# Two attention layers: context and query projections in half-precision parts, feed-forward tiles moved, and stacked queries and keys copied from tile to tile in SBUF

## The chip, the cores and the metric

The kernel runs on one core of one Trainium2 chip. The metric is the device time of one execution in microseconds. Engine names: TensorE (PE), VectorE (DVE), ScalarE (ACT), GpSimd (POOL), and SyncE (SP), which here only issues DMAs.

## What is computed

The batch has 64 sequences of 128 tokens, x with 320 channels and a context with 192 channels (its last 4 tokens are image tokens). Layer 0 is an attention with 8 heads of 40 channels, layer 1 a transformer block with 20 heads of 16:

```python
# layer 0
query, keyt, valt = x @ Wq, enc @ Wk, enc @ Wv            # enc: the first 124 context tokens
hs = mha(query, keyt, valt, 8)                            # "first"
ca_q1 = einsum('btc,th->bch', ca, Wq_ca)[:, indices, :]   # ca: the last 4
ca_hs1 = mha(ca_q1, x, x, 8)                              # "ca"
ca_hs2 = mha(ca_hs1 @ Wq, ca @ Wk_ca, ca @ Wv_ca, 8)
x = (hs + ca_hs2) @ Wout + b_out + x
# layer 1
h = ln(x);  x = attn(h, h, q1, k1, v1, 20) @ o1_w + o1_b + x          # "self"
h = ln(x);  x = attn(h, context, q2, k2, v2, 20) @ o2_w + o2_b + x    # "cross"
h = ln(x);  a, g = split(h @ ff_w1 + ff_b1)
out = a * gelu(g) @ ff_w2 + ff_b2 + x
```

## The kernel before

A step works on G = 2 sequences (256 tokens). It is one pass of a hardware loop (`Fori(0, STEPS + 1)`, 33 passes) on each engine, and the passes are software-pipelined: while pass i does the "ca" and self-attention of tile i, its cross-attention and the "first" attention, it also does the feed-forward part (`ff0` to `ff9`, `y0`, `y1`) of the tile before. After the loop a tail does the last tile's feed-forward part.

**The order is written out by hand**, once for each engine, and checked against one list of jobs, `BODY`. A job is one use of a PSUM bank: job n uses bank n mod 6 (`j_bank`), TensorE may fill it once the last reader of job n - 6 is done (`bank_free`), ScalarE reads it first, then VectorE (`a_done`, `v_done`). Two more banks (`o_bank`) hold the attention outputs.

Names of jobs: `Q0T0..2`, `K0T0..2`, `K1T`, `Q1T`, `Q2T`, `K2T` are chunks of transposed queries and keys for the first, self and cross attention; `V0`, `V1`, `V2` values; `S0..S27` scores of four heads each, `mx0..7` the turned maxima of a group, `T0..T27` the exponents (transposed scores with the maxima subtracted). Units 0 to 3 are "ca" (two for each sequence), 4 to 13 self, 14 to 23 cross, 24 to 27 first. For each `T` ScalarE computes two exponentials (in float32 to `P`, and in float16 to `PT`), GpSimd the low half `PT[1] = P - PT[0]` (`low_probabilities`, L519), and `attend` multiplies both with the values. `outT`/`outM` are the turned outputs and the output projection, `XT` the turned norm (`hTn`, `hT3` in the code, written by `high_blocks` L699 and `low_blocks` L1051 to L1054), `G` the token gains, `mT`/`mB` the extremes of the next tile over all partitions, `s4`, `p4T`, `hs` the small attention over 4 tokens, `caT` its turned queries.

**Precision.** Most matmuls multiply float16 parts: a value is split in a high half (ScalarE) and a low half, and `PASSES` lists eight products of 128 rows or fewer that cover 320 input rows. The projections from x (`Wq`) and from the context (`Wk`, `Wv`, `k2`, `v2`) are float32 matmuls instead (`transposed`, `values`), three input chunks for x and two for the context. A float32 matmul shows as two instructions in the trace.

**Stacking.** Scores need the high and low halves of queries and keys stacked on the partitions, one block of 16 or 40 rows for each part and one column block for each head (`Qs`, `Ks`, `Q0s`, `K0s`). The chunks `cQ` and `cK` are laid out otherwise. So SP stores each chunk to DRAM (`put`, L371) and, after the last chunk of a tensor, loads the stack back in three DMAs (`stack`, L375):

```python
def put(src, k, r, dst, at, landed):
    sp.dma_start(dst[:, at:at + r, :].rearrange("a p n -> p a n"), src[0:r, :, k, :]).then_inc(landed, 16)

def stack(dst, src, e, parts, landed):
    for y, part in enumerate(parts):
        sp.dma_start(dst[y * e:(y + 1) * e, :, :],
                     src[part, :, :].rearrange("(h e) n -> e h n", e=e)).then_inc(landed, 16)
```

Scores of a group wait for its whole stack (`self_stacked`, `first_stacked`, `cross_stacked`). SP also loads the next tile (`load_next`), in its place in one queue.

**The start** finds the largest weight (a maximum and a minimum of each matrix on VectorE), scales and splits the weights, computes bias shifts (`ff_shifts`: 20 tiles), and computes for all tiles the products of `Wk_ca` and `Wq` (`M4`), which go to DRAM in one DMA from ScalarE's queue. VectorE then clears buffers that lie over the staging area, and the loop begins.

## Time and profile before

| | us |
|---|---|
| median of 3 runs | 3950.0 (3941.24 to 3958.27) |
| the profiled execution: time | 3965.49 |
| its span, first to last instruction | 3963.6 |
| TensorE busy | 3580.9 (90%) |
| VectorE, ScalarE, GpSimd busy | 2308.9 (58%), 2268.7 (57%), 1966.4 (50%) |
| mean granted TensorE clock | 0.966 |

The busy time of TensorE includes modelled ends of pipelined matmuls, so what a group of matmuls costs is read from the start of the group to the start of the next. The span is read in three parts: the start, the 33 passes, the tail.

### The profile page before, as it was taken

The page shows a single profiled execution, that of the slowest core. Times are in us where ns is not written, and L with a number is a line of the kernel's source. Part 1 is how long each engine was busy: PE and PEld are TensorE (multiplying, and loading weights), DVE is VectorE, ACT ScalarE, POOL GpSimd, SP SyncE. Part 2 cuts the span into 40 slices and gives each one's busy share as a digit, 9 for nine tenths or more (in the row PEclk, how much of TensorE's full clock was granted, in tenths as well). Part 3 has the DMA queues.
Part 4 walks back from the last instruction along what each step waited for, and adds up shares of the span by engine and source line. Part 5 has one row for each costly group of instructions (what it writes and reads, how often), then busy time and mean ns, then how long its engine had stood idle before and what let it go on. Part 6 is the DMA issues. An engine that isn't in the chain of part 4 may idle for free.

```text
span 3963.6 us, 112057 instructions
## 1 busy us (share of the span) xinstructions
PE 3580.9 (90%) x38314; PEld 2867.6 (72%) x38314; DVE 2308.9 (58%) x5535; ACT 2268.7 (57%) x4084; POOL 1966.4 (50%) x2229
## 2 busy tenths in 40 slices
PE   6499999999999999999999999999999999999999
PEld 5377777777777777777777777777777777777777
DVE  6466556556555655655556556555655656556555
ACT  2356655665556556556655665566566556655664
POOL 0345444554555445555554554545445555554553
PEclk9799999999999999999999999999999999999999
DMA  4332333222233332232333322233332232333321
GB/s 138 63 61 53 58 61 66 59 46 60 59 55 61 67 61 49 53 65 51 63 63 66 59 46 60 56 58 61 67 64 47 53 64 53 63 63 66 59 46 42
DMA packets 417600, 238.71 MB, mean 60 GB/s; under 512 B 44315, under 2 KB 416715, under 8 KB 416843
## 3 DMA queue, kind: packets, MB, share of 16 engines
q1 hardware_dynamic: 405317, 229.62, 29.6%
q8 instruction: 366, 6.00, 0.7%
q10 hardware_dynamic: 11910, 3.04, 0.3%
...
## 4 chain that ended last, share of the span: by engine, by line
PE 36%; issue 30%; POOL 17%; DVE 5%; SPq 4%; DMA 3%; ACT 3%; POOLq 1%; ACTq 0%; DVEq 0%
PE bank L1412 35%; POOL PT L519 10%; DMA xin<-in_x 3%; DVE mx L1025 2%; ACT PT L742 2%; POOL cQ L526 2%; POOL XA L496 1%; POOL cK L526 1%; SPq L365 1%; POOL rstd L566 1%; SPq L363 1%; POOL XB L496 1%; PE bank L1446 1%; PE bank L1531 1%; SPq L361 1%
## 5 line engine op out<-in xcount | busy, mean ns | idle before, releaser
L519 POOL TENSOR_TENSOR PT<-P,PT 128x512 f16<-128x512 f32 (+1 forms) x924 | 1068.8, 1157 | 642.1 <-ACT PT L742 640.8
L1412 PE MATMUL bank<-hT,w_ff_w 128*128 128x256 f16 x5440 | 651.6, 277 | 1.7 <-DVE hT L1054 1.7
L1025 DVE TENSOR_REDUCE mx<-bank 128x4 f32<-128x512 f32 (+1 forms) x924 | 579.6, 680 | 104.4 <-PE bank L1412 96.5
L1412 PEld LDWEIGHTS bank<-hT,w_ff_w 128*128 128x128 f16 x5440 | 532.5, 100 | 73.2 <-issue 6.5
L1412 PE MATMUL bank<-mxs,pick 84*128 84x128 f16 (+1 forms) x3696 | 513.4, 220 | 0.0
L1412 PE MATMUL bank<-w_ff,F 128*128 128x320 f32 x1360 | 411.5, 442 | 1.3 <-DVE F L1104 1.3
L1412 PEld LDWEIGHTS bank<-mxs,pick 84*128 84x128 f16 (+1 forms) x3696 | 375.1, 103 | 16.8 <-issue 8.2
L1412 PEld LDWEIGHTS bank<-V,PT 128*128 128x128 f16 (+1 forms) x9504 | 314.5, 96 | 84.0 <-POOL PT L519 37.9
L723 ACT ACTIVATE P<-bank,ff_b,scale 128x256 f32<-128x256 f32 x340 | 187.8, 562 | 324.9 <-PE bank L1412 285.4
L1412 PE MATMUL bank<-Qs,Ks 96*128 96x128 f16 x2640 | 361.7, 220 | 0.1
L1412 PE MATMUL bank<-V,PT 128*128 128x17 f16 (+1 forms) x9504 | 343.7, 172 | 17.1 <-POOL PT L519 14.3
L1104 DVE SCALAR_TENSOR_TENSOR F<-bank,ff_b,P 128x256 f32<-128x256 f32 x340 | 163.3, 483 | 266.5 <-ACT P L723 262.7
L741 ACT ACTIVATE P<-bank,log_p,held 128x512 f32<-128x512 f32 x330 | 256.2, 776 | 80.7 <-PE bank L1412 42.8
L1412 PEld LDWEIGHTS bank<-w_ff,F 128*128 128x128 f32 x1360 | 242.4, 190 | 78.0 <-DVE F L1104 1.5
L565 POOL TENSOR_TENSOR rstd<-mv,eps 128x1 f32<-128x1 f32 x198 | 41.4, 209 | 502.8 <-DVE mv L1092 502.8
L741 ACT ACTIVATE P<-bank,log_p,exp_self 128x512 f32<-128x512 f32 x330 | 255.6, 775 | 45.0 <-PE bank L1412 42.8
L1412 PEld LDWEIGHTS bank<-Qs,Ks 96*128 96x128 f16 x2640 | 253.2, 98 | 20.9 <-issue 6.0
L1071 DVE RECIPROCAL rden<-bank 128x20 f32<-128x20 f32 (+1 forms) x264 | 63.2, 239 | 345.0 <-PE bank L1412 345.0
L526 POOL TENSOR_TENSOR cQ<-whole,cQ 128x256 f16<-128x256 f32 (+1 forms) x198 | 131.9, 667 | 257.8 <-DVE whole L929 254.2
L741 ACT ACTIVATE P<-bank,log_p,factor 124x512 f32<-124x512 f32 (+1 forms) x264 | 204.9, 776 | 93.4 <-PE bank L1412 87.7
L742 ACT ACTIVATE PT<-bank,log_p,held 128x512 f16<-128x512 f32 x330 | 254.6, 772 | 0.0
L742 ACT ACTIVATE PT<-bank,log_p,exp_self 128x512 f16<-128x512 f32 x330 | 254.4, 771 | 0.0
...
## 6 DMA issues: line engine op xcount, KB each, us to landing
Ks<-scratch_k SPq DMA_DIRECT2D x198, 160.0 KB, 4.5
Qs<-scratch_q SPq DMA_DIRECT2D x198, 160.0 KB, 5.7
...
Q0s<-scratch_q SPq DMA_DIRECT2D x99, 160.0 KB
K0s<-scratch_k SPq DMA_DIRECT2D x99, 160.0 KB
...
```

The lines of the kernel that those rows point to most:

```text
L361: sp.dma_start(cT2[0:r, k, :], d["cT"][before, k * r:(k + 1) * r, :]).then_inc(step_loaded, 16)
L496: nc.gpsimd.tensor_tensor(dst[:, b, :], src[:, b, :], bias[:, j, :], ALU.add).then_inc(ready, 1)
L519: nc.gpsimd.tensor_tensor(PT[0:keys, n % PT_SLOTS, 1, :], P[0:keys, n % P_SLOTS, :], PT[0:keys, n % PT_SLOTS, 0, :], ALU.subtract).then_in ...
L526: nc.gpsimd.tensor_tensor(dst[0:r, 1, k, :], whole[0:r, m % 3, :], dst[0:r, 0, k, :], ALU.subtract)\
L565: link(i, nc.gpsimd.tensor_tensor(rstd[:, j, b:b + 1], mv[:, j, b, 1:2], eps[:, :], ALU.add))
L723: nc.scalar.activation(gate[:, t % 2, :], bank[:, 0:GS], ACT.Gelu, scale=scale[:, 1:2], bias=ff_b[:, FFT + t:FFT + t + 1]).then_inc(a_done, 1)
L741: nc.scalar.activation(P[0:keys, n % P_SLOTS, :], bank[0:keys, :], ACT.Exp, bias=log_p[0:keys, :], scale=by)
L742: nc.scalar.activation(PT[0:keys, n % PT_SLOTS, 0, :], bank[0:keys, :], ACT.Exp, bias=log_p[0:keys, :], scale=by).then_inc(a_done, 1)
L1025: nc.vector.tensor_reduce(mx[:, g % 2, 4 * u:4 * u + 4], bank[:, :].rearrange("p (h s) -> p h s", h=4)[:, :, 0:keys], axis=AX.X, op=ALU.ma ...
L1071: link(i, nc.vector.reciprocal(rden[:, g % 4, 0:heads].unsqueeze(2), o[:, :, e:e + 1]))
L1104: nc.vector.scalar_tensor_tensor(out=F[:, t, :], in0=bank[:, GS:2 * GS], scalar=ff_b[:, t:t + 1], in1=gate[:, t % 2, :], op0=ALU.add, op1= ...
L1412: return nc.tensor.matmul(o, lhsT, rhs, start=start, stop=stop)
```

## The change

- `Wq`, `Wk`, `Wv`, `k2`, `v2` become split float16 weights like the others (`MATS16`), with new pass lists of eight products for x and five for the context. x and the context of a tile are split on chip: ScalarE scales them in place and takes the high halves (`split_x`, `split_context`), GpSimd the low halves (`low_x`, `low_context`).
- `Qs`, `Ks`, `Q0s`, `K0s` are filled by DMAs from `cQ` and `cK` directly, chunk by chunk (`spread`), for all but the cross keys. The columns of `Wq`, `Wk`, `q1`, `k1`, `q2` are permuted on the host for that. Each chunk has a semaphore of its own; a score unit waits for the chunks that hold its heads, and ScalarE's write over a chunk of `cQ` or `cK` waits for the copies out of it.
- The orders change: `ff0` to `ff3` come before `T0` and `ff4` to `ff7` around the end of the self-attention; `gate` is a buffer of its own, no longer part of `P`; `K0T`, `K2T`, `V0`, `S`, `outM` and others move; SP loads the next tile after the copies of `Q1T` and before those of `K0T`.
- At the start: one reduction with absolute values for each matrix, the products `M4` earlier and in four parts, each written to DRAM by itself, buffers cleared by GpSimd, the loads for the token products first.

The core of the diff:

```diff
+PASSES_C = ((1, 0, 0), (3, 0, 0), (1, 1, 0), (2, 0, 1), (2, 1, 1))
+PASSES_X = ((1, 0, 0), (1, 1, 0), (4, 0, 0), (2, 0, 1), (2, 1, 1), (5, 0, 1), (3, 0, 2), (3, 1, 2))
...
 BODY = jobs_of("""
-    Q0T0 XT0_0 Q0T1 XT0_1 Q0T2 K1T0 K1T1 K1T2 Q1T0 Q1T1 Q1T2 S0 S1 V0_0 V1_0 mx0 S2 S3 T0 K0T0 T1
-    V1_1 mx1 K0T1 T2 S4 S5 S6 S7 S8 T3 vca mx2 S9 S10 T4 S11 S12 T5 S13 caT0 T6 mx3 T7 T8 caT1 K0T2
-    T9 T10 T11 T12 T13 V0_1 outT1_0 ff0 ff1 outM1_0 outT1_1 ff2 ff3 outM1_1 XT1_0 ff4 s4 XT1_1 ff5
-    Q2T0 Q2T1 Q2T2 ff6 ff7 mT ff8 mB ff9 S14 S15 S16 S17 y1 S18 S19 mx4 S20 S21 S22 T14 S23 K2T0 T15
-    mx5 S24 T16 S25 T17 T18 T19 T20 S26 T21 mx6 T22 outT2_0 S27 y0 T23 p4T T24 mx7 T25 outM2_0 K2T1
-    T26 hs0 T27 outT2_1 V2_0 outT0_0 hs1 K2T2 outM2_1 outT0_1 XT2_0 V2_1 outM0_0 outM0_1 XT2_1 G
+    Q0T0 XT0_0 XT0_1 S0 Q0T1 Q0T2 K1T0 K1T1 K1T2 Q1T0 Q1T1 Q1T2 S1 ff0 S2 S3 ff1 ff2 mx0 K0T0 ff3 T0
+    V1_0 K0T1 mx1 K0T2 V0_0 T1 V1_1 T2 S4 S5 S6 S7 S8 T3 vca mx2 S9 T4 S10 T5 S11 T6 S12 S13 caT0
+    mx3 T7 T8 T9 T10 T11 T12 T13 caT1 ff4 outT1_0 ff5 ff6 ff7 outT1_1 outM1_0 outM1_1 ff8 XT1_0 ff9
+    XT1_1 s4 Q2T0 Q2T1 Q2T2 mT mB V0_1 K2T0 K2T1 y1 S14 S15 S16 S17 S18 mx4 S19 S20 T14 S21 T15 S22
+    S23 T16 S24 S25 mx5 T17 S26 T18 S27 mx6 T19 T20 T21 T22 p4T T23 T24 mx7 outT2_0 T25 y0 T26
+    outM2_0 V2_0 outT2_1 T27 hs0 outM2_1 outT0_0 hs1 XT2_0 V2_1 outT0_1 outM0_0 K2T2 outM0_1 XT2_1 G
...
+            def spread(name, k, dst, src, e, rows, parts):
+
+                heads = rows[k] // e
+                at = rows[0] // e * k
+                for y, part in enumerate(parts):
+                    sp.dma_start(dst[y * e:(y + 1) * e, at:at + heads, :], src[0:rows[k], part, k, :])\
+                        .then_inc(stacked[name][k], 16)
...
-            def put_low(i, name, k, src, rows, dst, at, landed, behind=None):
+            def put_low(i, name, k, dst, src, parts):
+                if (name, k) == ("Q0T", 0):
+                    sp.wait_ge(j_full, done(i - 1, LOOP_JOBS.number("T27"), "J"))
                 sp.wait_ge(v_done, v_job(i, LOOP_JOBS, f"{name}{k}"))
-                if behind is not None:
-                    sp.wait_ge(behind, i * STACK_LOADS + STACK_LOADS)
-                put(src, k, rows[k], dst, at[k], landed)
+                spread(name, k, dst, src, D0, CH0, parts)
...
+            def low_x(i):
+
+
+                pool.wait_ge(x_high, i + 2)
+                nc.gpsimd.tensor_tensor(x16[:, 3:6, :], xT[:, :, :], x16[:, 0:3, :], ALU.subtract).then_inc(x16_ready, 1)
+
+            def low_context(i):
+
+                pool.wait_ge(c_high, i + 1)
+                nc.gpsimd.tensor_tensor(c16[:, 2:4, :], cT[:, :, :], c16[:, 0:2, :], ALU.subtract).then_inc(c16_ready, 1)
...
+            def split_x(i):
+
+                act.wait_ge(step_loaded, i * LOADS_STEP + 2 * LOADS_STEP)
+                act.wait_ge(next_ready, i + 2)
+                act.wait_ge(j_full, done(i, LOOP_JOBS.number("Q0T2"), "J"))
+                nc.scalar.activation(xT[:, :, :], xT[:, :, :], ACT.Copy, scale=next_factor[:, SX:SX + 1])\
+                    .then_inc(x_scaled, 1)
+                act.wait_ge(x_scaled, i + 2)
+                nc.scalar.activation(x16[:, 0, :], xT[:, 0, :], ACT.Copy, scale=lower[:, :])
+                nc.scalar.activation(x16[:, 1:3, :], xT[:, 1:3, :], ACT.Copy).then_inc(x_high, 1)
...
-                        pe.wait_ge({SELF: self_stacked, CROSS: cross_stacked, FIRST: first_stacked}[att],
-                                   i * STACK_LOADS + STACK_LOADS)
+                elif b == 0 and att != CA:
+
+                    per = CH0[0] // D0 if att == FIRST else CH1[0] // D1
+                    for c in range(-(-4 * u // per), (4 * u + 3) // per + 1):
+                        if att == CROSS:
+                            pe.wait_ge(stacked["Q2T"][c], i * STACK_LOADS + 2 * STACK_LOADS)
+                        else:
+                            for name in (("K0T", "Q0T") if att == FIRST else ("K1T", "Q1T")):
+                                pe.wait_ge(stacked[name][c], i * STACK_LOADS + STACK_LOADS)
```

## Rows read from the trace of the kernel before

**Rows 1.** The page: busy time, share of the span, and instructions of each engine.
```profile
PE 3580.9 (90%) x38314; PEld 2867.6 (72%) x38314; DVE 2308.9 (58%) x5535; ACT 2268.7 (57%) x4084; POOL 1966.4 (50%) x2229
```

**Rows 2.** TensorE in order of time: start, duration, line, operation, count, idle before.
```profile
152.12 2.91 PE L1412 MATMUL bank<-xT,w_Wq 120*120 120x256 f32 x6 [4.34 <-DVE G L942]
...
1989.07 1.56 PE L1412 MATMUL bank<-xT,w_Wq 120*120 120x256 f32 x6 [1.59 <-DVE hT L1054]
...
2035.42 0.46 PE L1412 MATMUL bank<-V,PT 128*128 128x17 f16 x12 [0.44 <-POOL PT L519]
...
2061.78 1.06 PE L1412 MATMUL bank<-Ks,Qs 96*128 96x128 f16 x16
...
2088.57 0.25 PE L1412 MATMUL bank<-Q0s,K0s 120*124 120x128 f16 x1
...
2102.47 1.56 PE L1412 MATMUL bank<-xT,w_Wq 120*120 120x256 f32 x6 [1.59 <-DVE hT L1054]
...
3930.92 17.63 PE L1412 MATMUL bank<-hT,w_ff_w 128*128 128x256 f16 x160 [1.68 <-DVE hT L1054]
```

**Rows 3.** What TensorE waited for: total us, times, longest.
```profile
PE bank L1412 <- POOL PT L519: 105.1, 99, 1.6
PE bank L1531 <- DVE mx L1025: 56.8, 126, 1.2
PE bank L1412 <- DVE hT L1054: 52.6, 33, 1.7
...
PE bank L1412 <- DMA Qs<-scratch_q: 9.3, 19, 1.3
```

**Rows 4.** Two neighbouring passes: length, busy time per engine, granted clock, DMA share, GB/s.
```profile
269.00:381.60 112.60, 104.03 (x1147) 83.33 (x1147) 67.07 (x163) 67.68 (x122) 59.21 (x67) 0.98 0.31 57
381.60:498.83 117.23, 106.97 (x1146) 84.74 (x1146) 67.15 (x163) 67.69 (x122) 59.23 (x67) 0.96 0.29 57
```

**Rows 5.** TensorE in order of time: groups of matmuls and what follows them.
```profile
2051.12 3.67 PE L1412 MATMUL bank<-hT,w_ff_w 128*128 128x256 f16 x32
2054.63 0.27 PE L1638 MATMUL bank<-ident,ext_wide 128*128 128x128 f32 x1
...
2067.94 1.08 PE L1412 MATMUL bank<-cT,w_k 96*128 96x256 f32 x4
2068.86 0.22 PE L1412 MATMUL bank<-Qs,Ks 96*128 96x128 f16 x1
...
2095.73 1.24 PE L1412 MATMUL bank<-w_v,cT 96*128 96x320 f32 x4
2096.81 2.34 PE L1412 MATMUL bank<-w_Wout,hTn 128*128 128x320 f16 x16
2099.05 0.54 PE L1446 MATMUL bank<-ident,OB 128*128 128x128 f32 x3
```

**Rows 6.** Groups of ScalarE's instructions: count, busy us, mean ns, idle before.
```profile
L741 ACT ACTIVATE P<-bank,log_p,exp_self 128x512 f32<-128x512 f32 x330 | 255.6, 775 | 45.0 <-PE bank L1412 42.8
...
L723 ACT ACT_TABLE_LOAD x34 | 43.6, 1283 | 0.6
```

**Rows 7.** Groups of GpSimd's instructions: the low half of the probabilities.
```profile
L519 POOL TENSOR_TENSOR PT<-P,PT 128x512 f16<-128x512 f32 x792 | 915.9, 1156 | 615.4 <-ACT PT L742 614.1
```

**Rows 8.** SP's queue in order of time: three DMAs of a stack.
```profile
2028.39 1.30 SPq L375 DMA_DIRECT2D Ks<-scratch_k  x3
```

**Rows 9.** DMA issues: count, KB each, median us from issue to landing.
```profile
Ks<-scratch_k SPq DMA_DIRECT2D x198, 160.0 KB, 4.5
```

**Rows 10.** TensorE, VectorE and GpSimd at the start, in order of time.
```profile
46.79 29.14 PE L1412 MATMUL bank<-ln_b,raw_ff_w 128*128 128x1 f32 x120
...
125.62 0.59 DVE L1236 MEMSET X<- 128x640 f32 x1 [35.61 <-DMA scratch_M<-M_all]
...
150.35 0.72 POOL L541 TENSOR_TENSOR X<-xin,next_factor 128x320 f32<-128x320 f32 x1 [149.91 <-ACT next_factor L761]
...
157.12 3.60 POOL L558 TENSOR_TENSOR ca_heads<-ca,mask_ca 96x2048 f16<-96x2048 f16 x1
```

More of the change, by code:

```diff
@@ L308, in build @@
         split_done = sem("split_done")
-        self_put, q0_put, k0_put = sem("self_put"), sem("q0_put"), sem("k0_put")
-        q2_put, k2_put = sem("q2_put"), sem("k2_put")
-        self_stacked, first_stacked, cross_stacked = sem("self_stacked"), sem("first_stacked"), sem("cross_stacked")
+        stacked = {n: [sem(f"{n}_stacked{k}") for k in range(3)] for n in ("Q0T", "K0T", "Q1T", "K1T", "Q2T")}
+        k2_put, cross_stacked = sem("k2_put"), sem("cross_stacked")
         vx_ready, ca_ready = sem("vx_ready"), sem("ca_ready")
@@ L1845, in _ @@
[L1845 to L1851 removed]
+                attend(i, 22)
+                exponents(i, 25)
+                ff_part(i, 0, 8, 10)
                 attend(i, 23)
                 exponents(i, 26)
[L1854 removed]
+                out_proj(i, 2, 0)
+                values(i, "V2", 0, "v2")
```

862 lines of the change are left out of this document (455 added, 407 removed).

## The prediction

> **What bounds the kernel now.** I read the page first, for the shares of the engines; then what TensorE waited for; then the trace in order of time for one tile, to see what each stretch of the loop hangs on; then the start. TensorE is busy 90% of the span, ScalarE and VectorE under 60%, GpSimd 50% [rows 1]. The first matmul of the loop starts at 152.1 us, the last tile's work ends where the tail begins, at 3930.9, and the span ends at 3963.6 [rows 2]. So the time is start 152.1, 33 passes of 3778.8 / 33 = 114.5 us, tail 32.7. The profiled execution took 3965.5 us, 0.4% over the median of 3950.0; the sum is made against it and scaled at the end.
>
> One pass, from 1989.07 to 2102.47, took 113.4 us [rows 2]. I cut it at three points where the reader can see the order of the work: the end of the self-attention's last product (2035.9: it starts at 2035.42 and the next group 0.4 later), the first cross score (2061.78), and the last exponents of the first attention, T27 (2088.57). That gives A = 46.8, B = 25.9, C = 26.8, D = 13.9 us. TensorE's waits [rows 3] are mostly on GpSimd's low half of the probabilities, 105.1 us in all or 3.2 per pass, on VectorE's maxima (1.7) and at the head of each pass on the bank that VectorE's split of hT empties (1.6). The wait for the stacked queries is small: 9.3 us in 19 waits.
>
> The clock matters too. Of two neighbouring passes with the same instructions one took 112.6 at a mean granted clock of 0.98 and the other 117.2 at 0.96 [rows 4]: in both TensorE is at 1.2 GHz for a part of the pass and at 2.4 for the rest, and passes differ by that part.
>
> **The change, part by part.** *Projections in half precision.* Per pass 21 single-precision matmuls of 256 columns (Wq 9, Wk and k2 6 each) and 8 of 320 (Wv, v2) go. Two of the first kind take 2068.86 - 2067.94 = 0.92 us, two of the second 2096.81 - 2095.73 = 1.08 [rows 5]. In their place come 8 half-precision matmuls for each chunk of Wq and 5 for the others. A 256-column one costs 3.51 / 32 = 0.11 us (2051.12 to 2054.63), a 320-column one 2.24 / 16 = 0.14 [rows 5]. So Wq gives 3 x (1.38 - 0.88) = 1.5, Wk and k2 6 x (0.92 - 0.55) = 2.2, Wv and v2 4 x (1.08 - 0.70) = 1.5: 5.2 us of TensorE per pass. At the busy share of 90% most of it counts where TensorE sets the pace, none where ScalarE does.
>
> *The splits that this needs.* ScalarE gets six copies over 768, 256 and 512, and 512, 256 and 256 elements. The exponentials cost 0.775 for 512 [rows 6]; that bounds the six from above at 3.9 us (2560 elements), and nothing bounds them from below but the same row without its fixed part; I take 3. GpSimd gets subtractions over 768 and 512 elements: at 1.156 for 512 [rows 7], 2.9 us. The context's split stands between two chunks of Q0T, where ScalarE has half of each chunk's 0.9 us free; x's stands in the ten us before the cross scores; GpSimd does one during the projections and one after its last probabilities. I charge 0 to 0.5 us.
>
> *Feed-forward tiles moved.* Four of the ten move ahead of T0, four to the end of the self-attention. They fill the holes in A, but Gelu and Exp now alternate twice in a pass: two table loads of 1.283 us more [rows 6]. One lies before the first exponential and is on the path, the other before exp4, where it delays the extremes by up to 1.3. The Trainium skill (ScalarE: Activation LUTs, What ACT_TABLE_LOAD costs) adds a drain of about 1.38 us to each load; this would make the two cost 5.3 us and the pass some 1.4 to 2.8 longer than I sum. The trace shows no such gap after a load here, so the row decides.
>
> *Stacking on chip.* For five of the six tensors 3 stores to DRAM and 3 loads of 160 KB, which land 4.5 us after issue [rows 9], become 9 copies. Their issue on SP costs 1.30 / 3 = 0.43 us each [rows 8], so 1.3 per chunk; their landing is not in the trace: between nothing and 4.5 us, and I take 2, since each is a small part of a stack. The chain is then: Q1T's first chunk lands some 15 us after the pass begins and S4 comes at 23; the last lands at 17.5. With 4.5 us it is 20: still hidden. ScalarE's overwriting of cQ now waits per chunk for Q0T's copies: at most 0.5. What it can give is bounded by the waits in [rows 3]: 9.3 us of 3965. On SP the loads of the next tile now stand behind the copies of Q1T and ahead of K0T's, waiting until about 30 us into the pass; K0T is wanted only in C, so this is hidden.
>
> *The pass after, stretch by stretch.* A: TensorE reaches T0 after 17.8 us (Q0T 2.6, six chunks of K1T and Q1T 5.7, four feed-forward tiles of 1.75 each, the rest scores and turns). From there ScalarE sets the pace: a table load 1.3, 14 pairs of exponentials, 1.37 apart in the trace, 19.2, eight small copies 3.1, a wait of 0.7 for the self-attention's first maxima, then GpSimd's 1.2, the last product 0.4 and 1.1 for T0 itself and the hops between engines: 44.8 in all, with five more feed-forward tiles (8.75 us) done. B: TensorE's work is 20.1 us (three feed-forward tiles instead of eight, but all ten parts of y1, V0_1 and two chunks of K2T), and new waits come: 1.2 for the bank of y1 behind Q2T2, 1.0 at the two matmuls of the extremes, which no longer have a tile between them, and 1.0 before out_proj: 23.3. C: mx4 now follows its scores at once; five maxima of 0.6 each and y1's result stand before it, so T14 starts 4.6 us after S14; then a hop of 0.5, 14 pairs 19.2, the copies 2.1, GpSimd late by 0.5 (its 10 us on the next tile's queries and values begin after the extremes), less the 2.7 from T27 to the end of its exponentials: 24.2. D, counted from T27: its exponentials end at 2.7, GpSimd at 3.9, the last product at 4.3, VectorE's share of it at 6.4, the turn at 6.8, two out_proj of 1.1 with the last chunk of K2T (0.6) between them at 9.6; VectorE is then 0.2 late for the second residual (1.3), and a norm (0.4) and the split of hT (0.7) bring the bank of Q0T0 at 12.2 against 13.9. Sum 104.5 against 113.4, at the sampled pass's clock. The mean pass was 1.1 longer than the sampled one; I keep that and 0.4 for the splits: 106.0.
>
> *The start.* Now the folded products are written to DRAM in one piece, and VectorE waits 35.6 us for them [rows 10]. After, this write goes in four pieces beside the reductions of the weights, and the matrices' minimum pass is dropped. What is left is: scale at about 48 as now; TensorE's twenty shifts of 29.1 us [rows 10] with a bias product to 81; VectorE's last bias 85; GpSimd clears 2.4, then values and queries 10.4 (150.35 to 160.72, [rows 10]), then x's low half 1.8: the first Q0T at 100. Today GpSimd does those 10.4 us while the loop has begun. Saved: 52 us, with 35 (the write alone) and 65 as bounds.
>
> *Sum.* 100 + 33 x 106.0 + 32.7 = 3631 us span, and 1.9 around it: 3633. Scaled by 3950.0 / 3965.5: 3619 us.
>
> **Rivals.** *Only TensorE's work shrinks* (20 in 100): the waits that the moved tiles fill come back elsewhere one for one, as B and C show the beginning of. Then a pass is 114.5 - 5.2 = 109.3, the span 3740, the time 3727. For it: B and C get 5 us of new waits by my own count. Against: A's holes are next to the exponentials, and four tiles go exactly there.
>
> *The clock no longer falls* (12 in 100): the mean pass loses about 114.5 - 112.6 = 1.9 us to it [rows 4]. If no wait of the new pass brings it down the pass is 106.0 - 1.9 = 104.1 and the time 3556. Against: waits of 2 us or more stay at mx4 and at the loop's end. The Trainium skill (TensorE: Matmul & The Clock Gate, Part 1) has the clock halved after idling; by that rule the holes filled in A decide, and the two passes above agree in direction.
>
> *ScalarE and GpSimd set every stretch* (4 in 100): then the 5.2 us are worth nothing and all that they are given is on the path: two table loads 2.6, splits 3, low halves 2.9, 8.5 us on 114.5. The loop grows by 280, less 52 from the start: 4177 us, slower. It decides from the point where more than 1.6 us per pass (52 / 33) stays exposed with nothing gained. Against: ScalarE waits for TensorE in B, at each feed-forward tile, and was 57% busy.
>
> *The stacking does not matter, or lands late* (8 in 100): the copies land after 8 us, nearly twice the 4.5 of a whole stack [rows 9]; then Q1T's banks are held 3 us, a pass is 109, the time about 3717. That the copies as such bring nothing is part of my forecast.
>
> My forecast's own case has 54 in 100, the remaining 2 an unchanged time. Its range is 3560 to 3690 (a pass from 104.2 to 108.1). The range for 8 in 10 takes in both neighbours: 3530 to 3750. A difference under 0.5% cannot be told from none here; faster has 94 in 100, within it 2, slower 4.
>
> **What would show it.** The first Q0T at about 100 us; a period of 106; single-precision projections gone and TensorE's work down by 5 us a pass; waits of TensorE on GpSimd's PT and on mxs before T1 gone; mx4 waiting 2.6 us and y1's first part 1.1; four table loads a pass; the waits on the stacking below 10 us in all. Wrong would be: a wait on the copies or on K2T's store in front of the scores, a start later than 115, or TensorE waiting all through C more than the exponentials' 1.37 apart explains.

## The result, and the profile after

The changed kernel takes 3752.95 us (median of 4 runs, 3751.69 to 3754.52), against 3950.0 for the one before: ratio 0.9502, 95% interval 0.9481 to 0.9522. The forecast was 3619 us with a range of 3530 to 3750: the direction is right, the gain of 197 us is 60% of the forecast's 331, and the time lies just above the range. One execution of r2b_dram (4406 us) and one of r5_b (9303 us) stand far apart from the others of their kernels and are left out of all comparisons below.

The page of the changed kernel, the line of shares and the transfers:

```profile
PE 3433.0 (92%) x38842; PEld 2823.0 (75%) x38842; DVE 2282.8 (61%) x5540; ACT 2431.1 (65%) x4362; POOL 2082.5 (56%) x2307
...
Qs<-cQ SPq DMA_DIRECT2D x402, 64.0 KB, 2.6
Ks<-scratch_k SPq DMA_DIRECT2D x99, 160.0 KB, 4.9
```

Against [rows 1] TensorE has 148 us less to do and a larger share of a shorter span. A copy from tile to tile lands 2.6 us after its issue (forecast: 2, bounds 0 to 4.5). TensorE of the changed kernel in order of time, the edges that [rows 2] shows of before:

```profile
109.54 1.32 PE L1487 MATMUL bank<-x,w_Wq 128*120 128x256 f16 x5 [15.71 <-POOL x L587]
...
1532.97 1.08 PE L1487 MATMUL bank<-x,w_Wq 128*120 128x256 f16 x8 [0.72 <-DVE hT L1133]
...
1577.80 1.05 PE L1487 MATMUL bank<-V,PT 128*128 128x17 f16 x36
1578.70 0.49 PE L1487 MATMUL bank<-hT,w_ff_w 128*128 128x256 f16 x3
...
1603.03 1.28 PE L1487 MATMUL bank<-Ks,Qs 96*128 96x128 f16 x20
1606.83 0.39 PE L1609 MATMUL bank<-ident,mx 128*20 128x128 f32 x1 [2.52 <-DVE mx L1104]
...
1607.89 0.29 PE L1487 MATMUL bank<-Qs,Ks 96*128 96x128 f16 x1
...
1629.72 0.25 PE L1487 MATMUL bank<-Q0s,K0s 120*124 120x128 f16 x1
...
1642.21 1.08 PE L1487 MATMUL bank<-x,w_Wq 128*120 128x256 f16 x8 [0.72 <-DVE hT L1133]
...
3717.60 1.58 PE L1487 MATMUL bank<-hT,w_ff_w 128*128 128x256 f16 x13 [0.81 <-DVE hT L1133]
```

The start is 109.5 (forecast 100). The 33 passes take 3717.6 - 109.5 = 3608.1, 109.3 each (forecast 106.0); apart from the first (112.1) all take 109.2 to 109.5. The tail is 33.1. The sampled pass of 109.24 divides into A 45.7 (to 1578.70), B 24.3, C 26.7, D 12.5, against forecasts of 44.8, 23.3, 24.2 and 12.2. Of the 134 us between forecast and result the passes are 110, the start 9.5, and 14 the scaling by 3950.0 / 3965.5: this profiled execution (span 3750.7) is no slower than the other runs, so there was nothing to scale.

What TensorE waited for in the changed kernel, us in all, times, longest:

```profile
PE bank L1609 <- DVE mx L1104: 99.3, 99, 2.5
PE bank L1487 <- DVE whole L1005: 40.4, 33, 1.2
PE bank L1487 <- DVE diag L1044: 24.1, 33, 0.7
PE bank L1487 <- DVE hT L1133: 23.9, 33, 0.8
...
PE bank L1487 <- POOL PT L540: 11.9, 33, 0.4
...
PE bank L1487 <- ACT M_part L856: 10.8, 2, 10.3
```

Each new wait that the forecast named is there at nearly its price: mx4 2.5 a pass (forecast 2.6), y1's bank 1.2 (1.2), the diagonal 0.7 (1.0), around out_proj 0.6 in two waits (1.0). The wait on GpSimd's PT fell from 105.1 [rows 3] to 11.9, and no stack is waited for. So the list of TensorE's waits was right and the sum was not.

### The profile page after: what moved, and what is told of

The parts are those of the page before. It is cut to its first block, busy times and chain, and to the rows that moved or that the text cites. A ratio compares the mean times of both kernels' runs of the same rounds, so it can differ in the third digit from the quotient of the medians.

```text
span 3750.7 us, 114679 instructions
## 1 busy us (share of the span) xinstructions
PE 3433.0 (92%) x38842; PEld 2823.0 (75%) x38842; DVE 2282.8 (61%) x5540; ACT 2431.1 (65%) x4362; POOL 2082.5 (56%) x2307
## 4 chain that ended last, share of the span: by engine, by line
PE 35%; issue 29%; POOL 23%; DVE 8%; DMA 2%; POOLq 1%; ACT 1%; SPq 0%; DVEq 0%; ACTq 0%
PE bank L1487 32%; POOL PT L540 12%; POOL XB L517 2%; DVE mx L1104 2%; POOL cQ L547 2%; POOL cK L547 2%; DMA out<-X 2%; PE bank L1514 1%; POOL XA L517 1%; POOL rstd L598 1%; POOL c L592 1%; DVE OA L1219 1%; DVE hTn L1133 1%; POOL X L517 1%; DVE hTn L1130 1%
## 5 line engine op out<-in xcount | busy, mean ns | idle before, releaser
L1487 PE MATMUL bank<-hT,w_ff_w 128*128 128x256 f16 x5440 | 637.0, 272 | 0.8 <-DVE hT L1133 0.8
L1104 DVE TENSOR_REDUCE mx<-bank 128x4 f32<-128x512 f32 (+1 forms) x924 | 596.3, 683 | 56.1 <-PE bank L1487 49.4
L1487 PE MATMUL bank<-mxs,pick 84*128 84x128 f16 (+1 forms) x3696 | 553.5, 230 | 0.0
L1487 PE MATMUL bank<-Qs,Ks 96*128 96x128 f16 x2640 | 404.0, 235 | 15.1 <-DVE mxs L1113 15.1
L1487 PEld LDWEIGHTS bank<-mxs,pick 84*128 84x128 f16 (+1 forms) x3696 | 395.8, 109 | 4.1
L794 ACT ACTIVATE gate<-bank,ff_b,scale 128x256 f32<-128x256 f32 x340 | 187.5, 566 | 304.3 <-PE bank L1487 228.5
L1183 DVE SCALAR_TENSOR_TENSOR F<-bank,ff_b,gate 128x256 f32<-128x256 f32 x340 | 159.7, 478 | 251.8 <-ACT gate L794 250.4
L1487 PEld LDWEIGHTS bank<-Qs,Ks 96*128 96x128 f16 x2640 | 275.3, 106 | 29.3 <-DVE mxs L1113 20.9
L1005 DVE TENSOR_SCALAR whole<-bank,q_factor,qk_b 128x256 f32<-128x256 f32 (+1 forms) x297 | 160.5, 541 | 188.5 <-ACT cQ L723 167.1
L1113 DVE SCALAR_TENSOR_TENSOR mxs<-bank,mxs 20x128 f16<-20x128 f32 (+1 forms) x264 | 74.4, 282 | 310.4 <-ACT mxs L784 306.2
```

What stands on the lines that cost most here:

```text
L794: nc.scalar.activation(gate[:, t % 2, :], bank[:, 0:GS], ACT.Gelu, scale=scale[:, 1:2], bias=ff_b[:, FFT + t:FFT + t + 1]).then_inc(a_done, 1)
L1005: nc.vector.tensor_scalar(whole[0:r, m % 3, :], bank[0:r, 0:GS], q_factor[0:r, :], qk_b[0:r, c + k:c + k + 1], ALU.mult, ALU.add).then_inc ...
L1104: nc.vector.tensor_reduce(mx[:, g % 2, 4 * u:4 * u + 4], bank[:, :].rearrange("p (h s) -> p h s", h=4)[:, :, 0:keys], axis=AX.X, op=ALU.ma ...
L1113: nc.vector.scalar_tensor_tensor(out=mxs[MAX_LOW:MAX_LOW + heads, g % 2, :], in0=bank[0:heads, 0:S], scalar=2.0 ** -MAX_EXP, in1=mxs[0:hea ...
L1183: nc.vector.scalar_tensor_tensor(out=F[:, t, :], in0=bank[:, GS:2 * GS], scalar=ff_b[:, t:t + 1], in1=gate[:, t % 2, :], op0=ALU.add, op1= ...
L1487: return nc.tensor.matmul(o, lhsT, rhs, start=start, stop=stop)
```

## The experiments

Sixteen kernels were built on the changed one. "Pass" is (span - 33.1 - first Q0T0) / 33; the first Q0T0 comes at 108.0 to 109.6, but at 106.1 in r3, 111.6 in r5, 93.8 in r9, 93.5 in r13 and 95.7 in r15.

| run | what | us, median | ratio to before, interval | pass |
|---|---|---|---|---|
| (changed) | | 3753.0 | 0.9502 (0.9481 to 0.9522) | 109.3 |
| r1_fill | 9 useless matmuls before mx4 | 3718.8 | 0.9423 (0.9408 to 0.9439) | 108.3 |
| r2b_dram | stacks by way of DRAM | 3774.5 | 0.9551 (0.9524 to 0.9579) | 110.2 |
| r3_poolq | products' writes on GpSimd | 3747.1 | 0.9492 (0.9476 to 0.9508) | 109.3 |
| r4_putback | 5.3 us of matmuls put back | 3867.6 | 0.9801 (0.9785 to 0.9818) | 112.8 |
| r5_b | order of B | 3716.9 | 0.9402 (0.9375 to 0.9430) | 108.2 |
| r6_a | T2, S4 before V1_1 | 3773.3 | 0.9551 (0.9529 to 0.9572) | 110.0 |
| r7_by1 | y1 behind S15 | 3902.6 | 0.9882 (0.9817 to 0.9948) | 114.0 |
| r8_a | V0_0 behind T3 | 3865.2 | 0.9791 (0.9766 to 0.9816) | 112.7 |
| r9_start | three edits of the start | 3742.1 | 0.9486 (0.9461 to 0.9510) | 109.5 |
| r10_nogelu | Gelu left out, so no table loads | 3713.7 | 0.9412 (0.9388 to 0.9435) | 108.2 |
| r11_bfill | r5 and 11 useless matmuls | 3745.7 | 0.9493 (0.9469 to 0.9518) | 109.1 |
| r12_mb | r11, mB and K2T earlier | 3677.9 | 0.9317 (0.9299 to 0.9336) | 107.1 |
| r13_all | r12, r9, V0_0 behind mx2 | 3690.0 | 0.9348 (0.9331 to 0.9365) | 107.9 |
| r14_splits2 | ScalarE's splits twice | 3801.6 | 0.9628 (0.9610 to 0.9647) | 110.8 |
| r15_best | r12 and r9 | 3667.2 | 0.9288 (0.9272 to 0.9304) | 107.2 |
| r16_half | r12 with 5 useless matmuls | 3702.3 | 0.9378 (0.9357 to 0.9399) | 107.8 |

**r1_fill: is the lower clock what C lost?**

```diff
                 bank = j_next(i, LOOP_JOBS, f"mx{g}")
+                if g == 4:
+                    for _ in range(9):
+                        mm(bank[:, 0:512], w16["k1"][:, 0, 0, 0:128], w16["ff_w1"][:, 0, 0, 0:512])
                 v_job_done(i, LOOP_JOBS, f"S{LAST_UNIT[att, b]}")
```

> The changed kernel with nine half-precision matmuls of 512 columns put in front of the turn of mx4, into the bank that this turn overwrites; their results are used by nothing. They fill TensorE's wait of 2.5 us there and change no other wait. In every pass the records show TensorE at 1.2 GHz for 6.8 us right behind that wait. Theory 1, the lower clock is what C lost against the forecast: if all of it were on the path the pass falls by 3.4 us and the time to about 3640; counted by ScalarE's idle time in C (first exponentials 1.15 us after T14 instead of 0.6, then 0.3 to 0.8 in two places) about 1.3 us a pass, time about 3710. Theory 2, C is set by ScalarE's exponentials alone: no change, 3753 within 0.3%. Theory 3, the dip comes from something other than the wait: it stays where it is, and the time too. The first exponentials' distance from T14 and the granted clock in C show which.

Three stretches of C in the changed kernel, from S14 to mx4 and twice 6.83 us from there: length, busy time of each engine, granted clock, DMA share, GB/s:

```profile
1603.03:1606.83 3.80, 1.28 (x22) 1.11 (x20) 3.74 (x7) 0.00 (x0) 3.72 (x3) 0.95 0.00 0
1606.83:1613.66 6.83, 6.83 (x75) 6.68 (x76) 4.76 (x8) 4.74 (x9) 5.62 (x8) 0.53 0.01 2
1613.66:1620.49 6.83, 6.83 (x117) 6.23 (x115) 3.06 (x8) 6.56 (x11) 5.39 (x5) 1.00 0.01 2
```

The same in r1_fill:

```profile
1588.88:1592.68 3.80, 3.23 (x30) 1.90 (x29) 3.75 (x7) 0.00 (x0) 3.72 (x3) 1.00 0.02 4
1592.68:1599.51 6.83, 5.58 (x91) 4.89 (x92) 5.21 (x10) 5.38 (x11) 6.19 (x8) 1.00 0.00 0
```

In the second row of the first block TensorE is busy all of the time and gets 75 matmuls done at 1.2 GHz; in r1_fill it gets 91 done at 2.4 GHz and has 1.25 us to spare. In the changed kernel the records show 1.2 GHz for 6.8 us behind this wait in every pass, in r1_fill in none: filling the wait keeps the clock up. But the time falls by only 34 us, 1.0 us a pass: the small price of theory 1. ScalarE shows why. Its first exponential comes 1.15 us after T14's first matmul in the changed kernel and 0.75 in r1_fill, and it then idles 0.11 and 0.32 us between pairs, which r1_fill does not have; these make 0.8 of the 1.0. Behind the first exponential ScalarE's pairs set the pace, and TensorE's slower matmuls are hidden behind them.

**r2b_dram: what are the copies worth?** The five tensors go by `put` to DRAM and are stacked from there whole, as before the change.

```diff
-                for y, part in enumerate(parts):
-                    sp.dma_start(dst[y * e:(y + 1) * e, at:at + heads, :], src[0:rows[k], part, k, :])\
-                        .then_inc(stacked[name][k], 16)
+                put(src, k, rows[k], s_of[name], rows[0] * k, put_done[name])
+            def restack(i, name, dst, e, parts, head=0):
+                sp.wait_ge(put_done[name], i * CROSS_STORES + (1 + head) * CROSS_STORES)
+                stack(dst, s_of[name], e, parts, stacked[name][0])
```

> The changed kernel with the five stacks again by way of DRAM: three stores, then three loads of the whole tensor, one semaphore for each tensor, the columns of the weights in their first order. Forecast's theory, the copies bring nothing by themselves: within 0.5% of 3753, since S4 comes 23 us into the pass and the stack of Q1T would land at about 20. Rival, they matter at Q2T: its last part is split at 1594.3 in the pass from 1532.97, S14 starts at 1603.0; a store of 2 us, three issues and a load of 4.9 bring it to about 1602.5, and then to 0.5 to 2 us late if the queue is held up: up to 66 us, 3820.

22 us slower; the intervals just part. SP and then TensorE of r2b_dram at S14:

```profile
1714.33 2.41 SPq L396 DMA_DIRECT2D scratch_sQ2T<-cQ  x3
1718.21 1.33 SPq L400 DMA_DIRECT2D Qs<-scratch_sQ2T  x3
```

```profile
1724.59 1.29 PE L1496 MATMUL bank<-Ks,Qs 96*128 96x128 f16 x20 [0.38 <-DMA Qs<-scratch_sQ2T]
```

S14 comes 70.6 us into this pass and 70.4 to 71.0 into the others (mean 70.7), against 70.1 with the copies in every pass: 0.7 us later, at Q2T and nowhere else, for A is 44.8 us to its last attend in both. The other 0.2 us of the longer pass goes with the clock: in 8 of 32 passes the stretch at 1.2 GHz in C lasts 10.2 instead of 6.8 us. The rival holds. The forecast let the copies bring nothing, because it held them against the 9.3 us of waits in the kernel before; but there four feed-forward tiles lay between Q2T and S14, and the same change that moved them away made the landing matter.

**r4_putback: what is a microsecond of TensorE worth?** Matmuls into the same bank ahead of the real ones.

```diff
+                again(bank[0:rows[c], 0:GS], wn, src, at[c], rows[c], passes[0:5 if src is x16 else 3])
                 transposed16(bank[0:rows[c], 0:GS], wn, src, at[c], rows[c], passes).then_inc(j_full, 1)
```

> The changed kernel with matmuls put in front of the projections and the values of the context and of x, into the same banks, which the real ones then overwrite: 5 more for each chunk of Wq, 3 more for each chunk of Wk and k2 and for each of Wv and v2. By the trace of the kernel before this is 3 x 0.55 + 6 x 0.33 + 4 x 0.42 = 5.3 us of TensorE a pass, what the single-precision ones cost more. Theory: TensorE sets most of the pass, and these are worth nearly their whole time, 4.5 to 5.3 us a pass: 3900 to 3930. Rival, ScalarE sets A and C, where four of the thirteen lie in A and three in C and D: 2 to 3 us a pass, 3820 to 3850.

115 us, 3.5 a pass, between the theory and its rival. TensorE of r4_putback at the head of a pass, at T0, at A's last attend and at S14:

```profile
1576.37 1.63 PE L1487 MATMUL bank<-x,w_Wq 128*120 128x256 f16 x13 [0.61 <-DVE hT L1133]
...
1595.88 0.22 PE L1487 MATMUL bank<-ca_heads,G 96*128 96x128 f16 x1
...
1623.04 1.05 PE L1487 MATMUL bank<-V,PT 128*128 128x17 f16 x36
...
1649.34 1.28 PE L1487 MATMUL bank<-Ks,Qs 96*128 96x128 f16 x20
```

By stretch, against the pass of the changed kernel from 1532.97 (T0 at 1550.75, A's last attend at 1577.80, S14 at 1603.03): up to T0 2.0 us were put in, K0T0's three among them, and 1.7 came out (17.8 to 19.5); from T0 to A's last attend 1.1 in and 0.1 out (27.05 to 27.16); from there to S14 1.1 in and 1.1 out (25.23 to 26.30); in C and D 1.2 in and 0.5 out. So TensorE sets nearly all of the time before T0 and in B, another engine that of A behind T0, and C and D lie between.

**r5_b: are the waits of B on the path?**

```diff
-    ... Q2T2 mT mB V0_1 K2T0 ...
+    ... Q2T2 mT V0_1 mB K2T0 ...
-                ff_part(i, 1, 0, 4)
                 extremes_turned(i, L)
+                values(i, "V0", 1, "Wv")
+                ff_part(i, 1, 0, 4)
                 extremes_everywhere(i, L, 2)
```

On VectorE `extremes_context` moves ahead of Q2T's splits and `softmax4` behind `diagonal`, on ScalarE V0_1's copy ahead of `next_factors`.

> The changed kernel with the order around the extremes changed in B: VectorE takes the context's extreme before it splits Q2T and the softmax of the four tokens after the diagonal, and TensorE does V0_1 between the turn of the extremes (mT) and y1's first part, which then lies in front of mB. TensorE's waits of 1.22 us for y1's bank and 0.73 at the diagonal should both go. Theory, these two new waits are on the path as the forecast charged them: 1.8 to 1.9 us a pass, 3753 - 62 = 3691. Rival, C's start hangs on the chain of extremes, next_factors and K2T's splits on ScalarE and VectorE (last split at 1602.42, 0.6 before S14), and what TensorE gains is waited for again at mx4: under 0.7 us a pass, 3730 to 3753, with mx4's wait longer than 2.52.

Both waits went (1.22 to 0.28, 0.73 to none) and B shortened by 2.0 us (25.2 to 23.3 from the last attend), but the pass by 1.1: mx4's wait grew to 2.9, T14 came 5.2 instead of 4.9 us after S14, and passes now took 107.4 to 108.9. Part of the loss is the clock: C grew by 0.85 us on average, 0.3 of it at T14. Between r1 and the passes of r11 at full clock, where the clock does not differ, the order of B is worth 1.2 us (108.3 to 107.1).

**r7_by1: real work in mx4's wait.** As r5, with `... K2T1 S14 S15 y1 S16 ...` and `ff_part(i, 1, 6, 10)` behind `scores(i, 15)`.

> As r5_b, and y1's last four parts moved from ahead of S14 to between S15 and S16, VectorE's result of y1 behind S15's maxima, ScalarE's split of x behind K2T's two copies. The 2.2 us of TensorE work now lie where it waited 2.5 us for mx4, so the wait falls under 1 us; the first run with useless matmuls there showed that the clock then no longer falls, which gave 34 us. Theory: the pass shortens by the 1.9 of the extremes' waits, 1.0 of the clock and up to 2.2 of the moved work, unless VectorE, which is free of K2T's splits only at about 1601.8, holds the maxima: 4.0 us a pass, 3753 - 132 = 3621, between 3590 and 3660. Rival, VectorE and ScalarE set this stretch: only the clock's part is gained, 3719.

A miss, from an oversight in the edit. y1 uses the bank of the job six before it, which now is V0_1's, and its first part, ahead of mB, waited until VectorE had emptied that. TensorE's waits, then ScalarE's, in r7_by1:

```profile
PE bank L1487 <- DVE V L1024: 106.2, 66, 3.0
...
PE bank L1487 <- POOL PT L540: 71.5, 62, 2.4
```

```profile
ACT next_factor L828 <- DVE size L1061: 198.1, 33, 6.6
```

mB came late, with it next_factors, GpSimd's values and T14's low half.

**r6_a and r8_a: what sets A behind T0?** r6 orders TensorE `T1 T2 S4 V1_1 S5 S6 S7 T3 S8`, the other engines accordingly.

> The changed kernel with A's order changed in one place: T2 and S4 ahead of V1_1, T3 ahead of S8 and of the second attend. In the trace ScalarE idles 0.92 us before T3's exponentials and 0.19 + 1.12 around mx2, together 2.2, where the forecast took 0.7; from T4 to T13 its pairs follow each other 1.36 apart with no idle time. Theory, ScalarE sets A from T0 on and this idle time is what A lost against the forecast: 0.8 to 1.3 us a pass gone, 3710 to 3727. Rival, TensorE's own order or GpSimd's low halves set A: the idle time moves to another exponential, 3745 to 3753.

20 us slower. VectorE of the changed kernel, then of r6_a, ahead of mx2:

```profile
1557.61 0.49 DVE L1024 SCALAR_TENSOR_TENSOR V<-bank,V 128x320 f16<-128x320 f32 x1 [0.73 <-ACT V L766]
1558.02 3.07 DVE L1104 TENSOR_REDUCE mx<-bank 128x4 f32<-128x512 f32 x5
```

```profile
1567.13 0.49 DVE L1024 SCALAR_TENSOR_TENSOR V<-bank,V 128x320 f16<-128x320 f32 x1 [1.38 <-ACT V L766]
1567.54 2.47 DVE L1104 TENSOR_REDUCE mx<-bank 128x4 f32<-128x512 f32 x4
```

The maxima before mx2 end 8.2 us after T0's first exponential (1552.90) in the changed kernel, 8.9 in r6 (1561.10), and A is 0.7 us longer to its last attend, in every pass. In 9 of 32 passes of r6 the clock does not fall in C, with the same wait of 2.5 us at mx4, and these take 109.0; the others take 109.8 to 110.6. So not ScalarE's pairs alone set A: between T1 and T4 it is VectorE's chain V1_1, five maxima, mx2. r8 took V0_0 out of that chain and put it behind T3 (`... S8 T3 V0_0 mx2 S9 T4 vca ...`).

> The changed kernel with V0_0 moved from ahead of T1 to behind T3, and vca from ahead of mx2 to behind T4. The run before showed A 0.7 us longer when VectorE's maxima of S5 to S8 began later, so not ScalarE's exponentials but the chain V1_1's low part (1557.61), five maxima (3.07 us), mx2, T4 sets A between T0 and T4. V0_0 costs VectorE 0.54 and ScalarE 0.41 ahead of V1_1. Theory: T4's exponentials come 0.5 to 0.9 us earlier, A as much shorter, 3753 - 23 = 3730 (3722 to 3737). Rival, from T1 on ScalarE or TensorE sets A: 3750 to 3760.

A miss. mx2's turn did come 0.4 us earlier after T0's exponential, but V0_0's copy and low part now stood ahead of mx2's on ScalarE and VectorE, and T4 waited:

```profile
1604.90 0.28 PE L1609 MATMUL bank<-ident,mx 128*20 128x128 f32 x1 [0.71 <-DVE mx L1104]
...
1606.44 0.23 PE L1487 MATMUL bank<-Qs,Ks 96*128 96x128 f16 x1 [1.04 <-DVE mxs L1113]
```

Behind it TensorE ran at 1.2 GHz in A too (in the sampled pass for some 7 us from 1606.6), where it is closer to setting the pace: A took 49.3 us to its last attend in this pass and 46.3 in the one before, where it ran at full clock.

**r3_poolq and r9_start: the start.** r3 moves the five `dma_start` of the products from `act` to `pool`; r9 has that, VectorE's extremes of five weights behind the scale, and GpSimd's `x_values` and `low_x` ahead of its wait on `low_ready`.

> The changed kernel with the five writes of the folded products issued by GpSimd, which idles there, and no longer by ScalarE. In the trace of the changed kernel ScalarE shows 10.9 us between two copies of products, in the issue of such a write, and TensorE waits 10.4 us for the next copy; the matrices' maximum is ready at about 47.5 and its turn on TensorE comes at 57.0. Theory: the turn comes at 47 to 48, the scale 9 to 10 us earlier, first Q0T0 at about 100 instead of 109.5, time about 3743. Rival: the writes' own landing, or TensorE's shifts of 29 us behind the turn, set the start anyway: 109 and 3753.

> The changed kernel with three changes of the start, none in the loop: GpSimd issues the writes of the products, VectorE takes the row of the maximum ahead of the five extremes of the raw weights, GpSimd does the values of x and x's low half ahead of its wait for VectorE's last bias and leaves the token queries behind it. With the first alone the turn of the maximum came at 45.1 but its row was used at 52.8, for VectorE stood in those extremes, and GpSimd's wait held the first Q0T0 for 15.7 us. Theory: scale at about 46 instead of 58, first Q0T0 at 93 to 98 instead of 109.5 (the forecast said 100), loop unchanged: 3737 to 3742. Rival: TensorE's 20 shifts of 29 us and the weights' halves on ScalarE and VectorE set it, and it comes at 104 or later: 3747.

ScalarE of the changed kernel, then GpSimd of r3_poolq, at the second write; then TensorE of the changed kernel ahead of the scale:

```profile
26.76 9.25 ACTq L862 DMA_DIRECT2D scratch_M<-M_part  x1
```

```profile
27.14 0.78 POOL L615 DMA_DIRECT2D scratch_M<-M_part  x1
```

```profile
57.03 0.27 PE L1769 MATMUL bank<-ident,amax_one_each 128*1 128x128 f32 x1
57.67 0.38 PE L1487 MATMUL bank<-amax_row,one_row 1*128 1x1 f32 x2 [0.37 <-DVE amax_row L1280]
```

The forecast's "scale at about 48 as now" failed first on ScalarE: between two copies it stood 10.9 us in the issue of two writes, TensorE's products waited 10.3, and the turn of the maximum was queued behind them. Of the two, the write of 720 KB took 1.51 us to issue (25.21), and the small one right behind it, 90 KB for the last entry, 9.25; on GpSimd they took 1.91 and 0.78. Why the small one stands so long on ScalarE is not shown. r3 alone was a miss: the turn came at 45.1, but VectorE's row of it reached TensorE only at 52.8, and GpSimd waited 17.1 us for VectorE's last bias, so that the first Q0T0 came at 106.1 and not at 100; the time fell by 6 us, and the intervals overlap. In r9 the last row above is at 46.00 and the first Q0T0 at 93.8. Of the 15.8 us that r9 gains to the first Q0T0, 11 reach the end (the intervals overlap; the traces show it), for the first pass then takes longer (115.7): ScalarE idles 11.5 us for the first copies of Qs.

**r10_nogelu and r14_splits2: the two terms on ScalarE.** r10 has `ACT.Identity` for `ACT.Gelu`, so it leaves out the gate's function and its results are not those of the reference; r14 does the four half-precision copies of x and c a second time, into a tile `twice`.

> The changed kernel with Identity in place of Gelu; the feed-forward gate is left out of the computation that way, in number and length of the instructions nothing else. All four table loads of a pass go, 4 x 1.283 us of ScalarE. The forecast put the load ahead of T0's exponentials on the path (1.3) and let the one ahead of exp4 delay the extremes by up to 1.3. Theory: 2.0 to 2.6 us a pass, 3667 to 3687. Rival 1, ScalarE's loads are hidden: under 0.5 us a pass, 3737 or more. Rival 2, each costs twice what its row says: 4 us a pass or more, 3620 or less. By the Trainium skill (ScalarE: Activation LUTs, What ACT_TABLE_LOAD costs), which adds a drain of about 1.38 us to a load, it would be this second rival.

> The changed kernel with ScalarE's four half-precision copies of x and of the context done twice a pass, the second time into a tile that nothing reads: 0.71 would stay single, the four are 0.51 + 0.40 and 0.51 + 0.61 = 2.0 us of ScalarE more. The forecast took the splits to cost 0 to 0.5 us a pass in all. Theory, they are hidden: 0 to 0.5 us a pass, 3750 to 3770. Rival, x's split lies on the chain next_factors, K2T's copies, maxima, T14 with its whole length, for there TensorE waited 2.5 us for the maxima: 1.1 us or more a pass, and half of the context's: 3790 to 3810.

Four loads, 5.1 us of ScalarE, are worth 1.1 us a pass, less than the theory and far from twice their rows: 1.0 in A and 0.5 in B, and 0.3 to 0.4 is lost again behind mx4. The splits are the opposite: 2.0 us more of ScalarE cost 1.5 us a pass. Where x's split stands, in r14_splits2, ScalarE and then VectorE:

```profile
1619.48 0.51 ACT L745 ACTIVATE twice<-xT,lower 128x256 f16<-128x256 f32 x1
1619.90 0.61 ACT L746 ACTIVATE twice<-xT 128x512 f16<-128x512 f32 x1
1620.42 0.49 ACT L747 ACTIVATE x<-xT,lower 128x256 f16<-128x256 f32 x1
1620.82 0.61 ACT L748 ACTIVATE x<-xT 128x512 f16<-128x512 f32 x1
1621.34 0.81 ACT L733 ACTIVATE cK<-bank,fixed 128x256 f16<-128x256 f32 x2
```

```profile
1621.82 0.88 DVE L1017 SCALAR_TENSOR_TENSOR cK<-bank,fixed,cK 128x256 f16<-128x256 f32 x2 [2.61 <-ACT cK L733]
1622.62 0.54 DVE L1196 SCALAR_TENSOR_TENSOR X<-bank,scale,X 128x320 f32<-128x320 f32 x1
1623.08 3.07 DVE L1110 TENSOR_REDUCE mx<-bank 128x4 f32<-128x512 f32 x5
```

K2T's copies stand behind the split, VectorE's low part of K2T behind those, y1's result and C's first maxima behind that: T14 comes 5.7 to 5.8 us after S14 instead of 4.9. That is 0.9 of the 1.5. Most of the other 0.6 goes with the clock: in 14 of 32 passes the stretch at 1.2 GHz behind mx4 lasts 10.2 us, and C then takes 28.6 to 28.8 us against 27.4 to 27.9 in the rest. The context's half costs nothing: A is unchanged.

**r11, r12, r16: the clock again.** r11 is r5 with eleven matmuls in front of mx4. r12 puts mB between y1's second and third tile and, on ScalarE, K2T's copies ahead of `split_x`. r16 is r12 with five.

```diff
-                ff_part(i, 1, 0, 4)
+                ff_part(i, 1, 0, 2)
                 extremes_everywhere(i, L, 2)
+                ff_part(i, 1, 2, 4)
-                split_x(i)
                 high_chunk(i, "K2T", 0, cK, CH1[0], FK2)
                 high_chunk(i, "K2T", 1, cK, CH1[1], FK2)
+                split_x(i)
```

> The order of the second run's B (extremes early, V0_1 between mT and y1's first part) and eleven useless matmuls in front of mx4 together. Alone they gave 36 and 34 us. With that order TensorE waits 2.9 us at mx4 instead of 2.5, so the lower clock behind it should cost no less. Theory, the two are independent: 3753 - 36 - 34 = 3683. Since B alone gave 1.1 of 1.9 us and C ran at 1.2 GHz for longer there (clock 0.954 against 0.959), the fill may give up to 0.6 us a pass more: 3663 to 3683. Rival, both shift the same work and ScalarE sets C: 3700 or more.

> The order of r11 with mB after two of y1's first four parts instead of after all four, and ScalarE's split of x behind K2T's two copies. In r11's trace passes alternate between 107.06 and 111.35 us with the same waits; the longer ones have TensorE at 1.2 GHz for 9.8 us, which begins two us after a wait of 1.30 us for GpSimd's low half of T14. GpSimd is late because its queries and values begin only after next_factors. With mB 1.1 us earlier it should come in time. Theory: this wait falls under 0.3 us, no pass has the lower clock, all take 106.4 to 107.1: 109.5 + 33 x 106.8 + 33 = 3667, time 3655 to 3680. Rival: GpSimd's wait stays near 1 us and the clock falls in every other pass as before: 3735 to 3750.

> r12 with five instead of eleven useless matmuls in front of mx4: TensorE is kept at work for 1.1 us and waits about 1.3 us there. If any wait of more than a microsecond there brought the clock down, the pass would be 1.0 us longer, 3710; if it takes more than that (V0's and GpSimd's waits of 1.0 us in C did not bring it down in r12), every pass or most stay at 107.0: 3678 to 3690. In r11 a wait of 1.3 us for GpSimd brought it down in every other pass, which speaks for something between.

Two neighbouring passes of r11, then one of r12:

```profile
1419.62:1526.68 107.06, 100.94 (x1173) 81.14 (x1173) 67.37 (x163) 72.49 (x130) 62.26 (x69) 1.00 0.18 45
1526.68:1638.03 111.35, 105.23 (x1173) 84.59 (x1173) 67.46 (x163) 72.79 (x130) 62.08 (x69) 0.95 0.19 46
```

```profile
1502.89:1609.92 107.03, 101.16 (x1173) 81.07 (x1173) 67.55 (x163) 72.53 (x130) 62.11 (x69) 1.00 0.19 48
```

In r11 the counts are equal and one pass costs 4.3 us more than its neighbour at 1.2 GHz for some 10 us. Both have a wait of 1.30 us for GpSimd's low half of T14 ahead of it, so r11 missed its forecast by the clock. In r12 this wait was expected to go, and it does not: TensorE still waits 1.04 us at the same product, now for VectorE's maxima (31.1 us in 30 waits), while the waits for GpSimd fall from 54.8 to 15.1 us in all. But every pass but the first two takes 107.0 to 107.1, and the time is the one forecast. r16 leaves 1.43 us of waiting at mx4, and its passes mix 107.0 and 108.5. So the wait of 2.5 us at mx4 had a stretch at 1.2 GHz behind it in every pass of the changed kernel, but only in 23 of 32 in r6; waits of 1.3 to 1.4 had one in some passes and not in others; waits of 1.0 had none in r12, and one in 25 of 32 passes in r8's A. Shorter waits went with fewer such stretches in C, but the length of the wait alone does not decide; what else does is not shown.

**r13, r15: both together.** r13 is r12 with r9's start and V0_0 behind mx2, r15 the same without V0_0's move.

> As r12, and the three changes of the start of r9, and V0_0 moved to behind mx2, where ScalarE and TensorE wait, so that VectorE takes up the maxima of S4 earlier. r9 gave 11 us. V0_0 out of the chain ahead of T4 gave 0.4 us up to mx2 in the trace of r8, before it was lost behind mx2. Theory: 3667 - 11 - 13 = 3643, within 15 us. Rival: with the shorter A a wait turns up that brings the clock down, as in r8: 3680 or more.

> r12 with the three changes of the start alone, V0_0 where the changed kernel has it. In r13's trace a pass took 107.4 us instead of r12's 107.0, and every fourth or fifth took 109.9; the first Q0T0 came at 93.5 and the first pass then took 113.2. Theory, the start's changes leave the loop alone and V0_0's place brought both: 93.5 + 113 + 32 x 107.05 + 33 = 3665, time 3660 to 3672. Rival, the longer passes have to do with the start: 3685 to 3692.

V0_0 cost 0.3 us in A once more, and in the last two thirds every fifth pass took 2.5 us more, with TensorE at 1.2 GHz for 6.8 us in A. r15 has its first Q0T0 at 95.7, the first pass at 112.6, all others at 107.0 to 107.1. At 3667 us it beats both kernels, by 7.1% and 2.3%.

## Why the forecast was 134 us short

**Right.** T0 comes 17.8 us into the pass, as summed, with ScalarE's wait of 2.4 us a pass for Q0T's copies hidden (the forecast charged 0.5; a copy's issue takes 0.64 to 0.75 us of SP, not 0.43). The waits at mx4, y1 and the diagonal have nearly their forecast size. The engine that sets the pace was named rightly for B (TensorE) and, as far as r4 shows it, for A behind T0 (not TensorE): work put on TensorE costs its full length in B and 0.1 of 1.1 us in A. The allowance for the clock, 1.1, meets the 1.0 shown by r1, but by luck: it was the excess of the mean pass before over the sampled one, and what came is a stretch in C in every pass. Table loads: the Trainium skill (ScalarE: Activation LUTs, What ACT_TABLE_LOAD costs) adds a drain of about 1.38 us to each. In this trace the exponential starts within 0.02 us of the load's end (a load of 1.28 us from 1551.61, the exponential at 1552.90), so the row decided rightly. All four loads together, 5.1 us of ScalarE, were worth only 1.1 in r10: they were mostly hidden.

**The step that failed is the sum of A, B and C, each as the work of one pace-setter that hardly waits for another engine** ("From there ScalarE sets the pace"; "B: TensorE's work is 20.1 us"; "T14 starts 4.6 us after S14; then a hop of 0.5"). A +0.9, B +1.0, C +2.5, D +0.3 make 4.7 us, of which the allowances for clock and splits cover 1.5; the rest, 3.2 (3.3 by the mean pass), times 33 is the 110 us.

- A: the forecast gave ScalarE one wait of 0.7 between T0 and T13. It has 0.92 + 0.19 + 1.12, 1.5 more; other terms of this sum were about 0.6 too long. r6 shows what it waits for at T4: VectorE's maxima behind V1_1's low part.
- B: its waits are smaller than forecast (TensorE's together 2.8 against 3.2), so TensorE's own work was summed 1.4 us too low (21.5 for 20.1), and by r4 such work counts in full here. That the waits are on the path was right up to S14, which r5 brings forward by 2.0 us; of these only 1.1 reach the end of the pass.
- C: 1.0 is the clock (r1). At full clock T14 comes 4.75 us after S14, against 4.6, and its first exponential 0.75 after that, against 0.5. The largest single piece of the rest is one wait of ScalarE of 0.82 us ahead of T22's pair. TensorE, then ScalarE, of the changed kernel:

```profile
1618.36 2.94 PE L1487 MATMUL bank<-w_ff,F 128*128 128x320 f32 x10
```

```profile
1621.75 0.78 ACT L810 ACTIVATE P<-bank,log_p,held 128x512 f32<-128x512 f32 x1 [0.82 <-PE bank L1487]
```

  There are three buffers for PT (`PT_SLOTS = 3`), so T22's exponentials wait until T19's product is done. That product (1621.13 to 1621.58) stands behind ten matmuls of y0, 2.8 us, though its low half was ready at 1619.5. The forecast's C has no such wait. The gap is in r1, r12 and r14 too; no run moved y0, so what it is worth is not shown. A further 0.2 is a wait ahead of V2's copy.
- "ScalarE splits ... I charge 0 to 0.5 us": r14 prices a doubling of ScalarE's part at 1.5, 0.9 of it by a later T14 and most of the rest by the clock. What the first copy costs can't be read off it, and r12, which moves it behind K2T's copies, mixes that with mB.
- "That the copies as such bring nothing is part of my forecast": they are worth 0.7 to 0.9 us a pass (r2b: 22 us by the medians, 0.9 between the profiled executions).
- The start: "scale at about 48 as now" missed 10 us (57.7 instead of 48), of which 9.5 are left at the first Q0T0.

**The rival "only TensorE's work shrinks"** named the pass that came, 109.3 us, but not by its mechanism. r4 gives 3.5 us for the 5.3 that the projections save, not all; r2b adds 0.8. If these add up, the 5.2 us between 114.5 and 109.3 are these and about 0.9 for the order and the moved tiles, which no run isolates. The rival's time, 3727, misses the start and carries the same scaling. "The clock no longer falls" is wrong for this kernel and right for r12. Its ground was half right: with the holes of A filled, the clock no longer falls in A, where one began 17.6 to 22.0 us into every pass before; it falls 73.5 us into every pass, behind mx4's wait. "Stacking lands late" and "ScalarE and GpSimd set every stretch" did not come.
